# One decoder layer with a mixture of experts on one core: the final norm's groups dealt out anew over three engines, one wait moved, one chain of small steps split

## The reference

```python
x = _layernorm(x + _L0_attn_ref(x, w_in, w_out))
x = _layernorm(x + _L0_xattn_ref(x, ctx, ctx, Wq, ...))
# experts: N = 8192 tokens, E = 8, K = 2, cap = ceil(1.2 * N / E)
probs = softmax(x @ Wr + br); gates, ids = top_k(probs, K)
# per expert the cap assignments with the largest gates are kept
h = silu(einsum('ecd,edh->ech', xg, W1) + b1)
out = (einsum('ech,ehd->ecd', h, W2) + b2) * gate
y = zeros((N, D)).at[disp_tok].add(out)
x = _layernorm(x + y)
```

## Time and profile before

| | us |
|---|---|
| median of 3 runs | 1608.39 (1606.88 to 1608.49) |
| the profiled execution | 1605.66 |
| its span | 1603.9 |

### The profile page before, as it was taken

The page is one execution under the profiler, slowest core; times in us unless marked ns, Lnnn a source line. Parts: engine busy times, 40 slices in busy tenths (PEclk is TensorE's granted clock), DMA queues, the critical chain, the costliest instruction groups (busy, mean ns, idle before and its releaser), DMA issues. The chain is left out here.

```text
span 1603.9 us, 43834 instructions
## 1 busy us (share of the span) xinstructions
PE 1411.9 (88%) x17886; PEld 1186.8 (74%) x17886; DVE 1025.5 (64%) x2246; ACT 1011.0 (63%) x1549; POOL 622.0 (39%) x696
## 2 busy tenths in 40 slices
PE   8999999999999999999999581127999999999990
PEld 5777777777777777777777451026999999999980
DVE  5666666666677777777777556894455454454482
ACT  4677777777777777767777453265555565565544
POOL 2645444444542223232322100004455455455486
PEclk9999999999999999999999986558999999999995
DMA  6012222221122222222221173003433443443365
GB/s 193 24 59 61 62 61 61 62 61 48 55 62 68 81 81 81 76 77 65 79 81 42 62 224 70 0 1 109 96 71 76 95 103 48 99 103 50 90 232 192
DMA packets 115127, 130.73 MB, mean 82 GB/s; under 512 B 26634, under 2 KB 97068, under 8 KB 114928
## 3 DMA queue, kind: packets, MB, share of 16 engines
q1 hardware_dynamic: 100272, 106.18, 21.3%
q0 software_dynamic: 14656, 21.74, 7.6%
HBM read 83.73 MB, written 44.16 MB: 80 GB/s over the span
## 5 line engine op out<-in xcount | busy, mean ns | idle before, releaser
L515 ACT ACTIVATE at_pr<-at_A 128x2048 f32<-128x2048 f32 x128 | 240.7, 1881 | 145.7 <-PE at_A L335 145.7
L610 DVE TENSOR_REDUCE at_mx<-at_A 128x12 f32<-128x1536 f32 x128 | 224.6, 1755 | 56.9 <-PE at_A L300 53.3
L755 POOL TENSOR_SCALAR_AFFINE_SELECT at_pr<-at_pr 128x2048 f32<-128x2048 f32 x64 | 128.4, 2007 | 205.2 <-ACT at_pr L515 205.2
L1807 POOL DMA_INDIRECT total<-ex_o,ids x70 | 116.0, 1658 | 188.9 <-DVE ex_o L1740 173.9
L1688 DVE TENSOR_TENSOR ex_hT<-ex_h,ex_hT 128x384 fp32r<-128x384 f32 (+1 forms) x192 | 112.9, 588 | 95.7 <-ACT ex_hT L1628 82.6
L646 DVE TENSOR_TENSOR at_oT<-at_C,at_oT 128x512 fp32r<-128x512 f32 x64 | 44.3, 691 | 165.1 <-ACT at_oT L528 165.1
L1627 ACT ACTIVATE ex_h<-ex_U,ex_b 128x384 f32<-128x384 f32 (+1 forms) x192 | 116.8, 608 | 40.1 <-PE ex_U L35 33.1
L335 PE MATMUL at_A<-at_qp,at_kt 32*128 32x256 f32 x2048 | 139.8, 388 | 0.0
L350 PE MATMUL at_C<-at_pr,at_v 128*32 128x128 f32 x4096 | 138.4, 276 | 1.0 <-ACT at_oq L522 1.0
L350 PEld LDWEIGHTS at_C<-at_pr,at_v 128*32 128x32 f32 x4096 | 104.0, 109 | 43.3 <-issue 42.1
L35 PE MATMUL ex_D<-ex_w_even,ex_hT 128*128 128x256 f32 (+1 forms) x960 | 117.2, 281 | 1.0 <-DVE ex_raw L1735 0.9
(11 more groups left out here) (244 smaller groups left out, 3067.7 us busy)
## 6 DMA issues: line engine op xcount, KB each, us to landing
ex_w_in<-in_w SPq DMA_DIRECT2D x16, 1024.0 KB
at_turned<-in_x_turned SPq DMA_DIRECT2D x16, 512.0 KB, 4.5
at_x<-in_x SPq DMA_DIRECT2D x16, 512.0 KB, 3.9
x<-at_y SPq DMA_DIRECT2D x32, 256.0 KB, 2.4
at_x<-x SPq DMA_DIRECT2D x16, 512.0 KB, 3.9
at_turned<-in_ctx_turned SPq DMA_DIRECT2D x16, 512.0 KB, 4.6
rows<-at_y SPq DMA_DIRECT2D x32, 256.0 KB, 2.2
total<-at_y SPq DMA_DIRECT2D x32, 256.0 KB, 3.0
```

The lines of the kernel that those rows point to most:

```text
L515: nc.scalar.activation(pr[:, k % 2].rearrange("p i n a q -> p (i n a q)"), A[:].rearrange("p i n a q -> p (i n a q)"), ACT.Exp).then_inc(e ...
L610: nc.vector.tensor_reduce(mx[:, k % 2, 0:12], A[:, 0:3].rearrange("p i n a k -> p (i n a) k"), AX, ALU.max).then_inc(max_done, 1)
L755: nc.gpsimd.affine_select(out=t, in_=t, compare_op=ALU.is_ge, fill=0.0, base=0, pattern=[[0, 16], [1, P]], channel_multiplier=-1).then_inc ...
L1807: nc.gpsimd.indirect_dma_start(sum_dram, bass.IndirectOffsetOnAxis(ap=ids[0:n, e, at:at + 1], axis=0), o[0:n, pr, b, :], None, bounds_chec ...
```

## The change

Three things are changed, and the sums computed stay the same.

- Routing, head: ScalarE first makes an Exp of one column, then waits for the shifted logits and makes Exp; its wait for the constants is now behind Exp.
- Routing, end: the eight steps that make `ids` run first for the first expert's 10 columns and then for the other 70. GpSimd waits for the first, SP for both.
- The end: ScalarE normalises groups 0 and 1 inside the last expert, between the activations of its chunk 1 and chunk 2, and groups 4 to 13 as before; GpSimd groups 2 and 3; VectorE groups 14 and 15, behind all bulk statistics and ahead of the last own statistics. VectorE's statistics begin one group earlier (group 0 among the last four differences of chunk 1, group 1 ahead of the own rows) and are dealt out anew behind that. GpSimd gathers the own rows of chunk 1 only after the rates of group 1, and those of chunk 2 after normalising group 3. Own rates come after groups 6 and 9 where they came after 4 and 7.

```diff
         def _(act):
-            act.wait_ge(const_in, 160)
+            nc.scalar.activation(warm[:, 0:1], logits[:, 0, 0:1], ACT.Exp)
             act.wait_ge(routed, 1)
             nc.scalar.activation(pr[:, :, :], pr[:, :, :], ACT.Exp).then_inc(act_done, 1)
-            nc.scalar.activation(warm[:], dummy[:], ACT.Sign)
+            act.wait_ge(const_in, 160)
+            nc.scalar.activation(warm[:, 1:2], dummy[:], ACT.Sign)
...
-            link(v.tensor_copy(id_parts[:], bi[:]))
...
-            v.tensor_tensor(ids[:].rearrange("p e b -> p (e b)"), id_sum[:], empty[:], ALU.add).then_inc(ids_made, 1)
+            for first_row, end_row in ((0, LT), (LT, ROWS)):
+                rs = slice(first_row, end_row)
+                link(v.tensor_copy(id_parts[:, :, rs], bi[:, :, rs]))
...
+                v.tensor_tensor(ids[:].rearrange("p e b -> p (e b)")[:, rs], id_sum[:, rs], empty[:, rs], ALU.add).then_inc(ids_made, 1)
...
-POOL_GROUPS = 4
-OWN_AFTER = (4, 7)
+ACT_EARLY = (0, 1)
+POOL_GROUPS = (2, 3)
+DVE_GROUPS = (14, 15)
+OWN_AFTER = (6, 9)
...
+                if e == E - 1 and ch == 1:
+                    for g in ACT_EARLY:
+                        normalise_bulk(g)
...
-            def take_own(ch, bulk):
+            def take_own(ch, ahead, between):
                 e, j = E - 1, (E - 1) % 2
+                bulk_statistics(*ahead)
                 dve.wait_ge(own_in[ch], 16 * parts[ch])
...
+            def normalise_bulk(g):
+                dve.wait_ge(bulk_rates, g + 1)
+                for b in range(NB):
+                    t = g * NB + b
+                    ins = nc.vector.tensor_scalar(space(g)[:, b, :], space(g)[:, b, :], rstd[:, t:t + 1], shift[:, t:t + 1], ALU.mult, ALU.add)
+                ins.then_inc(bulk_made_dve, 1)
...
                     elif ch == 1:
-                        rest_h(e, j, ch)
-                        take_own(0, ((0, 4), (4, 8), (8, 12)))
+                        for m in range(HT):
+                            rest_h(e, j, ch, m, m + 1)
+                            if m >= HT // 2:
+                                bulk_statistics(m - HT // 2, m - HT // 2 + 1)
+                        take_own(0, (4, 8), ((8, 12), (12, 16), (16, 16)))
                         own_statistics(0)
                     else:
                         for m in range(HT):
                             rest_h(e, j, ch, m, m + 1)
-                            bulk_statistics(12 + m, 13 + m)
-                        take_own(1, ((20, 24), (24, 28), (28, 32)))
+                            bulk_statistics(16 + m, 17 + m)
+                        take_own(1, (24, 26), ((26, 30), (30, 34), (34, 38)))
                         own_statistics(1)
-                        take_own(2, ((32, 36), (36, 40), (40, 44), (44, tiles)))
+                        take_own(2, (38, 38), ((38, 42), (42, 46), (46, 50), (50, tiles)))
+                        for g in DVE_GROUPS:
+                            normalise_bulk(g)
                         own_statistics(2)
...
+            gather_own(0)
             pool.wait_ge(half_made, 1)
...
+                if g == ACT_EARLY[-1]:
+                    gather_own(1)
+                if g == POOL_GROUPS[-1]:
+                    gather_own(2)
```

More of the change, by code:

```diff
@@ L1014, in route_block @@
         key = sb("key", [P, F])
-        warm = sb("warm", [P, 1])
+        warm = sb("warm", [P, 2])
         limits = sb("limits", [P, 3])
@@ L1053, in route_block @@
             sem(n) for n in ("const_in", "dve_done", "pe_done", "act_done", "total", "tried", "split", "low_made"))
-        counted_dve, counted_act, counted_pool = (sem(n) for n in ("counted_dve", "counted_act", "counted_pool"))
+        counted_dve, counted_act = (sem(n) for n in ("counted_dve", "counted_act"))
         gates_stored, gates_made, ids_made = (sem(n) for n in ("gates_stored", "gates_made", "ids_made"))
@@ L1356, in sem @@
         return c.enter_context(nc.semaphore("ex_" + name))
-    sh = {name: sem(name) for name in ("w_in", "ident_in", "small_in", "t_full", "x_hi", "x_lo", "gate_ready", "chosen_ready",
+    sh = {name: sem(name) for name in ("w_in", "small_in", "t_full", "x_hi", "x_lo", "gate_ready", "chosen_ready",
                                        "w_hi", "w_lo")}
@@ L1428, in experts_block @@
         own_in = [sem(f"own_in{ch}") for ch in range(NC)]
-        bulk_stats, bulk_rates, bulk_made_act, bulk_made_pool = (
-            sem(n) for n in ("bulk_stats", "bulk_rates", "bulk_made_act", "bulk_made_pool"))
+        bulk_stats, bulk_rates, bulk_made_act, bulk_made_pool, bulk_made_dve = (
+            sem(n) for n in ("bulk_stats", "bulk_rates", "bulk_made_act", "bulk_made_pool", "bulk_made_dve"))
+        act_groups = [g for g in range(groups) if g not in POOL_GROUPS and g not in DVE_GROUPS]
         own_sum, own_stats, own_rates, own_made, own_stored = (
@@ L1528, in _ @@
             for g in range(groups):
-                if g < POOL_GROUPS:
-                    sp.wait_ge(bulk_made_pool, g + 1)
+                if g in POOL_GROUPS:
+                    sp.wait_ge(bulk_made_pool, POOL_GROUPS.index(g) + 1)
+                elif g in DVE_GROUPS:
+                    sp.wait_ge(bulk_made_dve, DVE_GROUPS.index(g) + 1)
                 else:
-                    sp.wait_ge(bulk_made_act, g - POOL_GROUPS + 1)
+                    sp.wait_ge(bulk_made_act, act_groups.index(g) + 1)
                 sp.dma_start(out_dram[g * G:(g + 1) * G, :].rearrange("(p b) n -> p b n", p=P), space(g)).then_inc(early_stored[g] if g < again else late_stored, 16)
@@ L1640, in normalise_own @@
                 ins.then_inc(own_made, 1)
[L1642 to L1648, removed]
+            for g in act_groups:
+                if g not in ACT_EARLY:
+                    normalise_bulk(g)
                 for ch in range(NC - 1):
@@ L1711, in own_statistics @@
                 ins.then_inc(own_stats, 1)
-            def take_own(ch, bulk):
+            def take_own(ch, ahead, between):
                 e, j = E - 1, (E - 1) % 2
+                bulk_statistics(*ahead)
                 dve.wait_ge(own_in[ch], 16 * parts[ch])
                 dve.wait_ge(gate_ready, e * NC + ch + 1)
+                wait(dve, own_sum, starts[ch])
                 for b, (_, n) in enumerate(tiles_of[ch]):
@@ L1719, in take_own @@
                     dve.wait_ge(d_full, at + 1)
-                    if b == 0:
-                        wait(dve, own_sum, starts[ch])
                     nc.vector.tensor_tensor(raw[0:n, b, :], Dn[(starts[ch] + b) % 2][0:n, :], b2[0:n, j, :], ALU.add).then_inc(d_done, 1)
@@ L1725, in take_own, with normalise_bulk @@
                                                    ALU.mult, ALU.add).then_inc(own_sum, 1)
-                    bulk_statistics(*bulk[b])
+                    bulk_statistics(*between[b])
+            def normalise_bulk(g):
+                dve.wait_ge(bulk_rates, g + 1)
+                for b in range(NB):
+                    t = g * NB + b
+                    ins = nc.vector.tensor_scalar(space(g)[:, b, :], space(g)[:, b, :], rstd[:, t:t + 1], shift[:, t:t + 1], ALU.mult, ALU.add)
+                ins.then_inc(bulk_made_dve, 1)
             def take_o(e, j, ch):
@@ L1819, in _, with gather_own @@
             sum_complete(pool)
-            for ch in range(NC):
+            def gather_own(ch):
                 free = (E - 1) * NC + ch
```

21 lines of the change are left out of this document (13 added, 8 removed).

## The result

| | before | after |
|---|---|---|
| median, runs side by side | 1607.46 us (11 runs) | 1602.46 us (11 runs) |
| ratio | | 0.9968, interval 0.9959 to 0.9977 |
| the profiled execution, its span | 1605.66, 1603.9 | 1602.73, 1601.0 |

The change makes the kernel 5.0 us faster, against 6.4 forecast. Because the stretch between routing and norm turned out to vary by itself, I compare the traces by distances between fixed marks. All marks are starts: the routing block's first instruction on GpSimd, the cast of the constants, the copy of the last product, TensorE's first product of the experts, SP's first bulk load, and the first scatter.

What follows compares the result with a forecast made beforehand. Bounds: VectorE's chain in routing; at the end ScalarE's normalising and the last store before the change, GpSimd's chain after it. Gains 2.7 + 2.1 + 1.6 = 6.4 us, so 1608.39 - 6.4 = 1602.0 us; range 1598.5 to 1606.5.

Steps and rivals of the forecast that it cites:

- rival (3): Last expert to first scatter: 1.6 us more on GpSimd cancels the gain there; routing's 4.8 stay: 1603.6 us, chance 0.12.
- Exp, 2.7: Routing head: Exp ahead of the constants' wait starts VectorE's casts 2.7 us earlier, until VectorE itself waits for the constants.
- warm-up Exp: Routing head: the one-column Exp fits ScalarE's idle time; costed at nothing, up to 1.4 us free.
- Ids, 2.1: Routing end: first expert's ids come 2.1 us earlier, and the block's end with them.
- 0.6 us of cover: Routing end: slack of VectorE's later remainders before its product of the gates; beyond it the ids' gain shrinks one for one.
- The last expert up to chunk 2: Last expert: early statistics and ScalarE's normalising of groups 0 and 1 fit into idle time; cost nothing.
- GpSimd's chain, 1.6: Last expert to first scatter: GpSimd's gathers, normalising and rates set the end; first scatter 1.6 us earlier.
- (1): Last expert, 1529 to 1549: VectorE shuts GpSimd out, gathers take 2.35 us, groups 3.46: 1612.7 us, chance 0.04.
- (2): Last expert: the eight loads land together at 1532, GpSimd's chain shifts by 7 us: 1609.0 us, chance 0.09.
- (4): GpSimd is quick: groups 2 and 3 at 2.18 us, first gathers unhindered, 1.3 and 0.6 more: 1600.1 us, chance 0.12.
- The two rules: Last expert: VectorE and GpSimd exclude each other for whole instructions; DMA completion is not FIFO per issuing engine. Both grounded rivals.

Runs made afterwards that it cites:

- early gathers: Changed kernel with chunk 1's own rows gathered right behind chunk 0's, instead of after the rates of group 1: ratio 0.9938 to the kernel before.
- pairs of rates: Changed kernel with last own statistics ahead of normalising groups 14 and 15, and rates of groups 4 to 13 made two groups per step: ratio 0.9988.
- both kernels with pairs: The paired-rates kernel (0.9988), and one adding chunk 1's gathers behind chunk 0's and first-expert weights' remainders behind the take of the gates (0.9947).

## Why the prediction was right, and where it was not

The forecast was 1602.0 us and the time is 1602.46. That is closer than the terms were: the gain was 5.0 us for 6.4, and the kernel before was 0.9 us quicker beside it (1607.46) than in the runs that I started from, which hid part of the error. So the nearness is in part luck: counted from this run's 1607.46, the forecast would be 1601.1 and rival (3), in which the tail gives nothing, 1602.7, and the time lies by the rival. Between the marks 4.1 us arrived (2.61 + 1.45 + 0). The remaining microsecond is no term of mine, and beside its parts the same change gave 4.2 us; the stretch of the experts, in which two traces of the changed kernel differ by 2.3 us, is large enough for the difference.

- **Exp, 2.7: right, 2.61.** The step that named the second wait for the same constant (VectorE's own) is what kept it from being 4.5. The warm-up Exp cost nothing.
- **Ids, 2.1: 1.45.** The ids came 1.61 us behind the copy, forecast 1.6, and the first gather 2.07 earlier. The failed step is the question "who waits for that": I followed VectorE's chain to the block's end and gave it 0.6 us of cover. The end belongs to GpSimd's sixth gather, 2.6 us ahead of TensorE's first product in nine traces, and VectorE had 1.6 us to spare in the kernel before. So 0.6 us of the 2.07 were lost, because the six gathers take 0.65 us longer: the third and fourth 2.40 and 1.90 beside the remainders, for 1.01, while the first and second, 2.35 and 1.61 before, are now 1.32 and 1.02. I had put this price on the first gather only, and as a gain.
- **The last expert up to chunk 2: right.** Statistics of groups 0 and 1 waited for no load and were done 8.7 and 10.4 us behind the first bulk load, forecast 8.6 and 10.4; ScalarE was 0.95 us early for chunk 2.
- **GpSimd's chain, 1.6: 0.** Right in kind: released by GpSimd's last rates behind VectorE's own statistics, not by a store, and shown by the early gathers to be on the path. Wrong in three small terms of the sum: rates of group 4 start 33.92 us behind the bulk load where 33.04 was forecast (+0.9; the two normalisings took 2.95 and 2.61, together what I had, but the rates of groups 2 and 3 took 2.3 and 2.6 for 2.0, and the first rates started 0.2 late), the 14 steps took 28.5 for 28.0 (+0.5), and VectorE's normalising of a group 1.38 for 1.13, with what follows (+0.3). Together 1.7 us, all of one sign: a long chain of small steps, most costed at the one duration that the rows showed, the undisturbed one.
- **What that chain could have told me.** I named GpSimd as the new bound and listed three gathers on it (4.5 us), but took their place as given. Costed as an edit of its own, their move behind the first rates is a loss of 4.5 us, since GpSimd has nothing else to do ahead of those; the runs say 4.4. That could be told from the rows of before.
- **Rivals.** (1), GpSimd shut out: it is there in sign, but small. The seven moved gathers took 1.01 to 1.22, not 2.35, and the groups 2.95 and 2.61. (2), loads together: fell, loads 0 and 1 were there at 1517.97 and 1521.89. (3), the tail gives nothing, 1603.6: this is what happened to the tail, for a longer list of reasons than both groups near 3.5. (4) fell.
- **The two rules.** For the Trainium skill's SBUF — State Buffer, "Who interferes with whom", the runs show: the third gather takes 2.40 us beside VectorE's two-input remainders and 1.01 once they are moved away, and a gather so held ends 0.88 or 0.89 us behind the end of the VectorE instruction it met, in agreement with a lock for a whole instruction. The rule was worth 0.6 us, in the routing, and next to nothing at the place where I feared it. The Trainium skill's "not FIFO per issuing engine", in DMA: Bandwidth & Descriptors, "Queues, rings and completion order", was the ground of rival (2), loads that land together and late. For groups 0 and 1 no statistic waits for its load, so nothing of the kind cost time here; whether the rule holds no run here shows.

## What to carry to other kernels

When a change makes another engine the bound, list everything it has moved onto that engine, transfers it issues included, and ask for each whether it stood in idle time before; here three gathers moved out of idle time ate the gain of taking four groups off ScalarE, and putting them back gave 4.4 us. At a barrier, look for the engine whose end always lies the same distance ahead of the next block, over several traces, before giving the block's end to the busiest one. A wait moved behind work gives only what lies between it and the next wait for the same thing. And before a slower version is put down to its idea, see where the time went: the pairs of rates lost most of theirs in a gap that no rate is in.

## What the runs showed of the hardware that I had not expected

- An indirect gather of GpSimd on 128 rows that starts beside one of VectorE's two-input instructions of 2.28 us ends 0.88 or 0.89 us behind the end of that instruction: 1.61 to 2.48 us in all, for 1.01 without (from the second gather of a block on), and this follows those instructions from the third to the sixth gather when they are moved.
- From the end of the last gather to TensorE's first product behind a barrier pass 2.6 us (2.59, 2.56, 2.61, 2.58; 2.53 to 2.63 in nine traces).
- GpSimd's small power step takes 0.88 us for 3 columns, 1.04 for 4 and 1.68 for 8: doubling the columns of a rate saves less than half.
- With the DMA engines full (share 1.0), a store of 0.5 MB took 6.3 us in the chain and a load 5.7 (rates in pairs), against 2.6 for the store at the end of the kernel.
- In both kernels with pairs GpSimd stands 2.7 and 2.9 us before its first scatter, behind the landing of the last store, waiting for nothing that the chain names, and 8 KB arrive there on the queue `q14 instruction`, in 0.42 and 0.53 us; in the eleven other traces neither is there.
